# A token tower in fp16 pieces on one core: a new order in steps 0 to 2 and in the last two projections, and an epsilon moved to VectorE

## The reference

```python
h = take(table, ids)                        # 64*256 = 16384 rows of 256 numbers
x = layernorm(h)                            # first norm
f, i, c = x @ Wf.T, x @ Wi.T, x @ Wh.T      # gates; then a scan over 256 steps of each sequence:
s = sigmoid(f) * s + sigmoid(i) * g(c)      # (written with logarithms in the original), s0 = 0.5
h = h + s
x = layernorm(h)                            # second norm
r = relu(ternary(w_fc)(x) + gate * x @ v.T @ fast_b.T @ u.T)     # 1024 wide, low rank 16
h = h + ternary(w_proj)(r * r)
```

## Time and profile before

| | |
|---|---|
| median of 3 runs | 910.86 us (910.43 to 911.01) |
| the profiled execution | 911.75 us, of which the span of the engines' work is 909.9 us |
| PE busy | 880.4 us, 97% of the span |
| ACT, DVE busy | 787.9 us (87%), 755.5 us (83%) |
| POOL busy | 416.5 us (46%) |
| chain that ended last, by engine | PE 89%, DVE 4%, ACT 3%, issue 2%, DMA 1%, POOL 1% |

### The profile page before, as it was taken

How to read it: one execution, slowest core, us unless ns; L and a number is a source line. 1 busy time by engine, 2 the same in 40 slices (tenths; PEclk the granted TensorE clock), 3 DMA queues, 4 the chain that set the end, 5 groups by cost and what they waited for, 6 DMA issues and landing times.

```text
span 909.9 us, 18335 instructions
## 1 busy us (share of the span) xinstructions
PE 880.4 (97%) x5505; PEld 483.1 (53%) x5505; DVE 755.5 (83%) x1338; ACT 787.9 (87%) x1195; POOL 416.5 (46%) x457
## 2 busy tenths in 40 slices
PE   4979999999999999999999999999999999999997
PEld 2435554555555455555455555545555555555554
DVE  5988888888888888888888888888888888888766
ACT  5677998888998888899888899888889988899884
POOL 7446544445544445554444554444555444433110
PEclk9989999999999999999999999999999999999999
DMA  5122534443343444243344334344424344432411
GB/s 146 24 53 66 93 74 87 99 100 57 82 81 74 98 98 75 70 89 73 85 98 98 58 81 82 74 98 98 77 73 85 77 82 98 99 64 70 77 46 47
DMA packets 179292, 72.88 MB, mean 80 GB/s; under 512 B 138694, under 2 KB 174096, under 8 KB 179264
## 3 DMA queue, kind: packets, MB, share of 16 engines
q1 hardware_dynamic: 173120, 68.33, 35.2%
q0 software_dynamic: 6144, 4.21, 2.1%
HBM read 27.68 MB, written 24.64 MB: 57 GB/s over the span
## 4 chain that ended last, share of the span: by engine, by line
PE 89%; DVE 4%; ACT 3%; issue 2%; DMA 1%; POOL 1%; SPq 0%; ACTq 0%; DVEq 0%; POOLq 0%
PE bank L847 34%; PE bank L869 24%; PE y_ps L783 23%; PE bank L883 4%; PE turned L823 1%; PE turned L760 1%; ACT relu L570 1%; PE turned L770 1%; ACT sq L583 1%; PE turned L771 1%; ACT normed L508 1%; DMA rows_raw<-table,idx_now 0%; DVE stats L1015 0%; DMA w_raw<-wh 0%; DVE hid L1276 0%
## 5 line engine op out<-in xcount | busy, mean ns | idle before, releaser
L869 PE MATMUL bank<-x_cols,fc_t 128*128 128x512 f16 x1024 | 245.1, 382 | 3.2 <-ACT relu L570 3.2
L419 POOL TENSOR_SCALAR var_eps<-moments 128x4 f32<-128x4 f32 x64 | 59.4, 928 | 387.8 <-DVE moments L1019 387.5
L847 PE MATMUL bank<-x_cols,w_hi 128*128 128x512 f16 x768 | 229.7, 381 | 3.4 <-ACT forget L559 1.9
L847 PE MATMUL bank<-x_cols,w_lo 128*128 128x512 f16 x768 | 229.3, 380 | 0.0
L783 PE MATMUL y_ps<-proj_t,sq_hi 128*128 128x256 bf16 x1024 | 225.6, 273 | 3.0 <-DVE sq_lo L1202 3.0
L783 PE MATMUL y_ps<-proj_t,sq_lo 128*128 128x256 bf16 x1024 | 225.6, 273 | 0.0
L570 ACT ACTIVATE relu<-bank,relu_scale 128x512 f32<-128x512 f32 x256 | 159.0, 688 | 39.8 <-PE bank L883 39.2
L409 POOL DMA_INDIRECT rows_raw<-table,idx_now x128 | 147.1, 1149 | 59.9 <-issue 31.4
L869 PEld LDWEIGHTS bank<-x_cols,fc_t 128*128 128x128 bf16 x1024 | 95.2, 98 | 131.1 <-issue 29.5
L1202 DVE TENSOR_TENSOR sq_lo<-sq,sq_hi 128x1024 f16<-128x1024 f32 x128 | 150.7, 1215 | 5.8 <-ACT sq L583 5.6
L508 ACT ACTIVATE normed<-h,shift,rstd 128x256 f32<-128x256 f32 x256 | 132.7, 601 | 5.2 <-POOL shift L427 5.2
(11 more groups left out here) (143 smaller groups left out, 918.8 us busy)
## 6 DMA issues: line engine op xcount, KB each, us to landing
out<-out_sb SPq DMA_DIRECT2D x31, 512.0 KB, 3.0
spill<-hid_blocks SPq DMA_DIRECT2D x30, 256.0 KB
hid_rows<-spill SPq DMA_DIRECT2D x120, 64.0 KB
rows_raw<-table,idx_now POOLq DMA_INDIRECT x128
x_cols<-x_rows SPq DMA_TRANSPOSE x120, 4.2
sq<-w_fc SPq DMA_DIRECT2D x1, 1024.0 KB
pj_raw<-w_proj SPq DMA_DIRECT2D x1, 1024.0 KB
out<-out_sb SPq DMA_DIRECT2D x2, 256.0 KB, 2.1
```

The costliest lines, as they stand in the source:

```text
L847: ins = pe.matmul(gate_bank(p, par)[:, :], w[:, k, q, :], x_part(0, par, part)[:, :, k, :], start=(k == 0 and w is w_hi and part == 0), st ...
L869: ins = pe.matmul(fc_bank(f, par)[:, :], fc_t[:, f, k, :], x_part(1, 0, part)[:, :, k, :], start=(opens and k == 0 and part == 0), stop=(n ...
```

## The change

It does the following, in the order of the diff below.

- Two semaphores more, `var_ready_first` and `sq_hi_last`, made behind all others.
- For the second norm of chunks 0 and 1, DVE adds epsilon and negates the mean in `measure`; POOL's `root` starts with the power.
- The last high square, pair 3 of chunk 31, is written by ACT from relu, where DVE copied it; the other three stay with DVE.
- In step 0, ACT sums w_proj between its first evictions, where it did so at the end of the step. PE runs `turn_low_rank` ahead of `gate(0)`, where it stood between `gate(0)` and `gate(1)`. DVE does `scale_low_rank` ahead of `cols_low(0)`, and `split_low_rank` behind `measure(0, 1)`; at the end of step 0 it does `guard`, `guard_sum` and `measure(0, 2)` (which was the first thing of step 1) and then `split_u`; `set_relu_scale` goes to step 1 behind `cols_low(1)`.
- In step 1, ACT does `normalise(0, 2)` ahead of `low_high(0)`, where it stood behind it, and puts off the two squares of the last pair to step 2, behind the four evictions of banks 0 to 2. In step 2 these four evictions go in the order forget, input, candidate, where candidate came first; the waits on `gate_taken` on PE and DVE follow this.
- In step 2, DVE does `part_low` ahead of `scale_output(0)`.
- `project(30)` and `project(31)` take the pieces one after the other, `high(p)` and `low(p)`, each with a wait for its own piece alone. `project(30)` runs high 0, high 1, low 0, high 2, low 1, high 3, low 2, then the transposes of chunk 31, then low 3.

```diff
@@ root (POOL)
-                pool.wait_ge(moments_ready[k], TILES * (c + 1))
                 wait(pool, normed_ready[k], TILES * c)
-                pass_on(pool, pool_passed, c)
-                pool.tensor_scalar(var_eps[k][:, :], ...)
-                pool.tensor_scalar(minus_mean[k][:, :], ...)
-                pool.wait_ge(var_ready[k], 2 * c + 2)
+                if known_below(c, 2) and isinstance(c, int) and k == 1:
+                    pool.wait_ge(var_ready_first, 2 * c + 2)
+                else:
+                    pool.wait_ge(moments_ready[k], TILES * (c + 1))
+                    pass_on(pool, pool_passed, c)
+                    pool.tensor_scalar(var_eps[k][:, :], ...)
+                    pool.tensor_scalar(minus_mean[k][:, :], ...)
+                    pool.wait_ge(var_ready[k], 2 * c + 2 - 4 * k)
@@ back and step (ACT)
                     square(m, 3)
+                    if not front:
+                        act.wait_ge(y_done, m)
+                        act.activation(sq_hi[:, 6:8, :], relu[:, 3, :, :], ACT.Square).then_inc(sq_hi_last, 1)
...
                     evict(0, par, 0, 0, forget, ACT.Sigmoid)
+                    sum_proj(0)
                     evict(0, par, 0, 1, inp, ACT.Sigmoid)
+                    sum_proj(1)
                     normalise(0, 1, h0[:, 1, :, :])
...
-                    act.wait_ge(pj_in, 16)
-                    for k in range(KD):
-                        act.activation(pj_a[:, k, :], ...)
...
                     part_high(0)
+                    normalise(0, 2, h0[:, 0, :, :])
                     low_high(0)
-                    normalise(0, 2, h0[:, 0, :, :])
                     x_high(0, 2)
-                    back(1)
+                    (back(1) without the squares of pair 3)
                     return
                 if second:
-                    evict_low()
+                    evict(2, par, 0, 0, forget, ACT.Sigmoid)
+                    evict(2, par, 0, 1, inp, ACT.Sigmoid)
+                    evict(2, par, 0, 2, cand_sig, ACT.Sigmoid)
+                    evict(2, par, 0, 3, cand_lin, ACT.Identity, 0.5)
+                    square_high(0, 3)
+                    square(0, 3)
@@ project (PE)
+                if isinstance(c, int) and c == N - 1:
+                    for p in range(3):
+                        high(p)
+                        low(p)
+                    high(3)
+                    for b in range(2):
+                        low(3, (2 * b, 2 * b + 1)).then_inc(y_done, 1)
+                    return
@@ gate and free (PE)
-                        pe.wait_ge(gate_taken, 8 * n + ((1, 2) if start else (4, 3))[p - 4])
+                        pe.wait_ge(gate_taken, 8 * n + ((1, 2) if start or second else (4, 3))[p - 4])
@@ measure (DVE)
+                if isinstance(c, int) and c < 2 and k == 1:
+                    dve.wait_ge(moments_ready[k], TILES * (c + 1))
+                    wait(dve, rstd_ready[k], c)
+                    dve.tensor_scalar(var_eps[k][:, :], ...).then_inc(var_ready_first, 1)
+                    dve.tensor_scalar(minus_mean[k][:, :], ...).then_inc(var_ready_first, 1)
@@ before step 0, step 0 and step 1 (DVE)
+            scale_low_rank()
             cols_low(0)
-            scale_low_rank()
             guard(1, 64, 1)
             guard_sum(1, 1)
-            split_low_rank()
             measure(0, 1, h0[:, 1, :, :])
+            split_low_rank()
...
                     residual(0, 0)
-                    split_u()
-                    set_relu_scale()
                     guard(2, 64, 0)
                     guard_sum(2, 0)
+                    dve.wait_ge(h0_ready, 3)
+                    measure(0, 2, h0[:, 0, :, :])
+                    split_u()
                     return
                 if first:
-                    measure_next()
                     cols_low(1)
+                    set_relu_scale()
                     part_low()
```

More of the change, by code:

```diff
@@ L733, in _ @@
             turn_normed(0)
+            turn_low_rank()
             def turn_bound():
@@ L789, in project @@
[L789 to L800, removed]
-                    return
@@ L802, in project, with tiles @@
[L802 to L806, removed]
+                def tiles(part, p, rows=range(TILES)):
+                    for f in (2 * p, 2 * p + 1):
+                        for j in rows:
+                            ins = pe.matmul(y_ps[:, j, :], part[:, f, j * P:(j + 1) * P], proj_t[:, f, :],
+                                            start=(f == 0 and j % 2 == 0 and part is sq_hi),
+                                            stop=(f == FC - 1 and part is sq_lo), skip_group_check=True)
+                    return ins
@@ new lines, in high, with low @@
+                def high(p):
+                    if isinstance(c, int) and c == N - 1 and p == 3:
+                        pe.wait_ge(sq_hi_last, 1)
+                    else:
+                        pe.wait_ge(sq_hi_ready, 4 * c + p + 1)
+                    return tiles(sq_hi, p)
+                def low(p, rows=range(TILES)):
+                    pe.wait_ge(sq_lo_ready, 4 * c + p + 1)
+                    return tiles(sq_lo, p, rows)
+                if isinstance(c, int) and c == N - 1:
[5 more added lines that the diff above has]
+                        low(3, (2 * b, 2 * b + 1)).then_inc(y_done, 1)
+                    return
@@ new lines, in project @@
+                if isinstance(c, int) and c == N - 2:
+                    high(0)
+                    high(1)
+                    low(0)
+                    high(2)
+                    low(1)
+                    high(3)
+                    low(2)
+                    turn_normed(1, N - 1)
+                    low(3).then_inc(y_done, 1)
+                    return
+                for p in range(4):
+                    pe.wait_ge(sq_hi_ready, 4 * c + p + 1)
+                    pe.wait_ge(sq_lo_ready, 4 * c + p + 1)
+                    for f in (2 * p, 2 * p + 1):
+                        for j in range(TILES):
+                            for part in (sq_hi, sq_lo):
+                                ins = pe.matmul(y_ps[:, j, :], part[:, f, j * P:(j + 1) * P], proj_t[:, f, :],
+                                                start=(f == 0 and j % 2 == 0 and part is sq_hi),
+                                                stop=(f == FC - 1 and part is sq_lo), skip_group_check=True)
@@ L896, in step @@
                         pe.wait_ge(x_landed[0], 32 * (n - 1))
-                    gate(0)
-                    if start:
-                        turn_low_rank()
-                    gate(1)
-                    gate(2)
+                    for p in range(3):
+                        gate(p)
                     if first:
@@ L1259, in weigh @@
                     if e == 0:
-                        dve.wait_ge(gate_taken, 8 * n + (2 if start else 3))
+                        dve.wait_ge(gate_taken, 8 * n + (2 if start or second else 3))
                     wait(dve, scanned, 4 * (n - 1) + 2 * e + 2)
@@ L1268, in scan @@
                     if e == 0:
-                        dve.wait_ge(gate_taken, 8 * n + (1 if start else 4))
+                        dve.wait_ge(gate_taken, 8 * n + (1 if start or second else 4))
                     if e == 0 and steady:
@@ L1370, in step @@
                     x_low(0, 3)
+                if second:
+                    part_low()
                 scale_output(n - 2)
-                part_low()
+                if not second:
+                    part_low()
                 if ahead and not second:
```

47 lines of the change are left out of this document (31 added, 16 removed).

## The result

In seven runs each, side by side, the changed kernel took 913.31 us (912.31 to 915.20) and the kernel before 911.09 (910.43 to 911.60): ratio 1.0024, with a 95% interval of 1.0015 to 1.0033. It is slower by 2.2 us, where 2.84 us less was forecast. The profiled execution took 912.61 us, its span 910.8.

What follows compares the result with a forecast made beforehand. PE is busy throughout 100 to 840 us, so only its waits before 97.40 and behind step 31 count. Head -2.4 and end -0.44 sum to -2.84 us: 908.0 us from the 910.86 median (908.9 profiled), range 906.5 to 909.3.

Steps and rivals of the forecast that it cites:

- Steps 3 to 31 issue the same instructions in the same order. 0.: Term for the steady loop: same instructions in the same order, so no change in time, 0 us.
- The head: Term for everything up to gate(0) of step 3: it starts at 95.0 in place of 97.40, -2.4 us.
- its 0.4 us in step 0: Step 0: moving split_low_rank behind the measurement takes 0.4 us off DVE's queue up to residual(0, 0).
- The epsilon on DVE: Behind the measurement of chunks 0 and 1: two small DVE instructions more, costing 0.3 us (0.2 to 0.4).
- The 0.5 us on POOL's side: POOL's power can begin some 0.4 us behind the moments in place of about 0.9, a gain of 0.5 us.
- the bound of 48: Sign of a wrong prediction: POOL's shift, before low_parts of step 1, ends behind 48 us.
- The end: Term behind step 31: project(31)'s last stretch has 20 matmuls in place of 24, -0.44 us (0.2 to 0.7).
- So 0: project(30): low_parts of step 32 still waits for cols_low, which hangs on ACT's normalise, so no gain, 0 us.
- the first rival: Around 51 us the clock does not fall, or for less; some 1.2 us come through, 906.8 us; chance 0.13.
- POOL's shift: Forecast to end at 47.0; rival: held beside DVE's guards until 48.5, losing 1.3 us, about 909.2 us; chance 0.10.
- wait for the transposes: Rival at step 3: fetches and transposes land no earlier, so gate(0) gains only 0.2 us; 910.2 us; chance 0.09.
- second stretch at 1.2 GHz: Rival in steps 1 and 2: a further 6.8 us at the slow clock costs 3.4 us; 911.4 us; chance 0.06.

Runs made afterwards that it cites:

- e5: Kernel before with five idle semaphore increments at the start of DVE's program; 911.53 us, ratio 1.0005.
- e6: Kernel after with three idle semaphore increments at the start of DVE's program; 908.63 us, ratio 0.9973.
- e2: Kernel after with the last two projections and the last high square as before, so only the edits of steps 0 to 2; 917.24 us, ratio 1.0064.
- e1: Kernel after with one wait more: POOL's gathers in the loop wait until DVE's value multiply is done; 908.97 us, ratio 0.9973.
- e3: Kernel before with only the new order of the last two projections and ACT's last high square; 910.25 us, ratio 0.9988.
- e4: Kernel after without the epsilon edit on DVE and POOL and its semaphore; 909.68 us, ratio 0.9980.
- e18: Kernel after, unchanged, run again as a control; 923.45 us, ratio 1.0128.
- e9: Kernel of e5 with POOL's root waiting for normed_ready ahead of moments_ready; 911.57 us, ratio 1.0003.
- e11: Kernel after with POOL's root waiting for moments_ready first again; 908.76 us, ratio 0.9975.
- e15: Kernel after with one idle semaphore increment at the start of DVE's program; 909.09 us, ratio 0.9974.
- e16: Kernel after with POOL clearing 1012 of the 1024 columns of rows_raw in the loop; 908.76 us, ratio 0.9974.
- e10: Kernel of e4 with five idle semaphore increments at the start of DVE's program; 909.60 us, ratio 0.9983.
- e17: Kernel of e5 with one idle increment on POOL ahead of the loop's gathers and 72 columns fewer cleared; 911.37 us, ratio 0.9998.
- e8: Kernel of e1 with eight idle increments on POOL ahead of the gathers of each loop step; profiled execution 910.02 us.
- e12: Kernel of e8 with 13 idle increments on POOL in place of 8; profiled execution 909.47 us.

## Why the prediction was wrong

**The step that failed** is "Steps 3 to 31 issue the same instructions in the same order. 0." The order was the same, but not the places of the instructions. Shown: the epsilon edit pushes DVE's loop back by five instructions (e5), a pause of 0.1 us then falls ahead of value (e5, e6), POOL's first gather wins in even steps, and in the group where that was compared, signals of low_parts came late with early gathers (e2) and not without (e1, e3, e4). Each costs up to 1.5 us, since the part pieces stand in a row behind it: ACT's part_high, DVE's part_low, low_sums. Measured, the term that was put at 0 is +3.86 us in the profile of the kernel after, +1.77 in e2 and +14.90 in e18. Not shown: why a signal of TensorE comes late beside an early gather, and what else it needs; e5, e9 to e11, e15 and e16 have the early gather and no late signal, all in groups of the other kind. The rule that the stretch "is as long as PE's own work" held only while every release came at once.

**The head.** gate(0) of step 3 at 95.23 against 95.0, so -2.17 for -2.4. The ways to it: low_parts of step 1 at 52.05 for 51.2, since DVE did not get its 0.4 us in step 0; bound_b took 1.69 us beside a gather and a clear of POOL, 0.28 before, and residual(0, 0) started 0.46 us later. cols_low started at 50.72 for 49.9. The epsilon on DVE took 0.18 us for 0.3. The 0.5 us on POOL's side came: its power began 0.36 us behind the end of the moments, where it was 0.89. But the moments ended 0.46 us later, so shift ended at 47.64, as before, where 47.0 was forecast; the bound of 48 held. The edit is worth 0.84 us of time by e11 against e10, which ran together.

The later marks lie near the forecast: gate(0) of step 2 at 65.84 for 66.0, x_low(1, 1) at 79.04 for 79.3, low_parts 83.39 for 83.7, low_sums 86.86 for 86.6. (The printed terms for this low_parts, 89.03 - 0.55 - 2.8 - 2.6, give 83.1; 83.7 is what the 86.25 of before less 2.6 gives.) This is in part luck. Low_parts of step 1 came 0.85 us late, and the way from it to gate(0) of step 2 took 13.79 us for a forecast 14.8, beside the shorter stretch at 1.2 GHz. The length of that stretch is not a thing of the change: with the head of before it is 6.8 us in before and e17 and 3.4 in e3, e5 and e9, with the head of after 3.4 in eight kernels and 6.8 in e8 and e12 to e15. The windows of e5 and of e8:

```profile
50.00:60.00 10.00, 6.78 (x32) 2.33 (x30) 7.24 (x20) 6.13 (x12) 6.67 (x10) 0.83 0.05 11
```

```profile
50.00:60.00 10.00, 8.13 (x30) 2.93 (x34) 7.21 (x21) 6.73 (x12) 7.30 (x10) 0.66 0.31 62
```

So the two profiles that give -2.17 have unlike stretches. Over all profiles low_parts of chunk 2 starts at a median of 112.6 in five kernels with the head of before and of 110.97 in 13 with that of after, so the head is worth rather 1.6 us; a single profile of it varies by 1.5. Among those with 3.4 us at 1.2 GHz the medians are 112.48 and 110.93, with 6.8 us 112.99 and 111.81: 1.2 to 1.6 us from the head at a like clock.

**The end** gave 0.86 us in all traces that have it, not 0.44: 0.62 behind low_parts of chunk 31, and 0.23 in project(30), which the step "So 0" denied. There PE got on with its high pieces and was waiting when cols_low ended, so that low_parts followed it by 0.05 us in place of 0.18; and cols_low itself ended 0.10 us earlier, counted from low_parts of chunk 30. e3 gives 1.2 us by the clock (0.3 to 2.0).

**The sum** without the loss is -2.46 in e6, -2.39 in e11 and -2.49 in e1, for -2.84. The mechanism was right there; head and end were off by 0.8 and 0.4 in opposite directions, so the sum lies nearer than its terms.

**The rivals.** The clock fell for half as long (0.83), as the first rival said; what it gave went into the late low_parts of step 1, as far as the two differences above tell, and low_sums of step 2 waited 1.24 us for part_low, so the 1.2 us on top of the forecast did not come. POOL's shift was neither at 47.0 nor at 48.5. gate(0) of step 3 shows no wait for the transposes. No second stretch at 1.2 GHz. The slower side was given to a mechanism in the head with 0.04; the one that came was in none of the cases, though the text says that waits of PE beyond 100 us would refute it.

## What to carry to other kernels

A stretch bound by one engine is only as safe as the signals that it waits for: look at how much slack a tight chain has (here some 0.16 us on the way from low_parts to low_sums), and at which transfers of POOL run beside it. An edit ahead of a loop moves the loop's code, and where two engines come within some 0.1 us of each other, as value and the gather here, that changes which of them is held; so compare who goes first in each pair, step by step, before you believe that an untouched loop costs nothing. Make such an order a wait (e1 cost nothing and had no late signal in its one group, where e2 had ten) rather than leave it to chance. And run the control in the same group as the cure.

## What the runs showed of the hardware

- A pause of 0.1 us, 0.35 the first time, at a fixed place of VectorE's program, counted in instructions, each time the loop comes by. The Trainium skill ("Advanced Engine Details and Errata", "Sequencer Memory") lists instruction caches with lines, and a rule of that kind would give such places; that a line's border is the cause no run here shows.
- A multiply that starts 0.02 us ahead of a gather in place of 0.13 leaves the gather at 1.15 us in place of 1.60, and each gather behind it comes 0.44 us earlier.
- TensorE's semaphore came 0.1 to 1.7 us late while its matmuls went on: ten times in the loop in each of three profiled executions and in no other, and worth 3.9, 1.8 and 14.9 us. The count's own record is as late as the instruction that waits for it.
- A trace can lack counts that took place: 137 to 159 of the spill's 480 are recorded in seven traces, all in the others, while a wait for all of them ends as early.
- The stretch at 1.2 GHz around low_parts of step 1 took 3.4 or 6.8 us, either length with either head.
- The same kernel took 913.31 us in one group and 923.45 in another, with each group within 3 us, while the kernel before stood at 911.09 to 911.56 in all of them.
